# Mixing products of sixteen-head attentions: 32 streamed columns of values in place of 64

## The reference

```python
scores = jnp.einsum('bhqd,bhkd->bhqk', q, k) / np.sqrt(dk)
attn = jax.nn.softmax(scores, axis=-1)
o = jnp.einsum('bhqk,bhkd->bhqd', attn, v)
o = o.transpose(0, 2, 1, 3).reshape(B, S, D) @ Wo
```

## Time and profile before

| what | value |
|---|---|
| median of 3 runs | 5153.12 us (5146.67 to 5158.76) |
| span of the profiled execution | 5152.4 us |
| own time of the profiled execution | not listed apart; span and median differ by 0.7 us |
| PE busy, share of the span | 4143.7 us, 80% |
| DVE, POOL, ACT busy | 2973.1, 2418.9, 2100.3 us |
| mean granted TensorE clock | 0.892 of full speed |
| all mixing matmuls (L719) busy | 766.1 us |

### The profile page before, as it was taken

How to read it: one execution, slowest core, us unless ns; L and a number is a source line. 1 busy time by engine, 2 the same in 40 slices (tenths; PEclk the granted TensorE clock), 3 DMA queues, 4 the chain that set the end, 5 groups by cost and what they waited for, 6 DMA issues and landing times. The chain is left out here.

```text
span 5152.4 us, 287025 instructions
## 1 busy us (share of the span) xinstructions
PE 4143.7 (80%) x120907; PEld 3282.4 (64%) x120916; DVE 2973.1 (58%) x10848; ACT 2100.3 (41%) x5737; POOL 2418.9 (47%) x4370
## 2 busy tenths in 40 slices
PE   7998987255799987656898997749878998889988
PEld 6887764133576776523777885425547887778866
DVE  4555548532344478787554553863335657776656
ACT  3554445111343445365454555112224543345622
POOL 3443432177333477587333442028874446655510
PEclk9999998655899989856999998869998999999989
DMA  3000001333100022200000001114431000000000
GB/s 90 5 5 18 18 16 54 75 65 61 38 0 0 11 38 38 38 1 1 1 0 10 19 19 50 41 40 76 76 61 32 0 9 18 17 10 1 0 10 25
DMA packets 380523, 139.90 MB, mean 27 GB/s; under 512 B 216486, under 2 KB 373238, under 8 KB 380054
## 3 DMA queue, kind: packets, MB, share of 16 engines
q1 hardware_dynamic: 345430, 107.60, 8.8%
q0 software_dynamic: 34816, 28.34, 3.8%
HBM read 91.46 MB, written 43.85 MB: 26 GB/s over the span
## 5 line engine op out<-in xcount | busy, mean ns | idle before, releaser
L1049 DVE TENSOR_REDUCE rowmax<-ps 128x16 f32<-128x1024 f32 x512 | 626.9, 1224 | 732.3 <-PE ps L676 732.3
L695 PE MATMUL ps<-qT,kblock 32*64 32x64 f32 x36864 | 946.5, 229 | 45.1 <-issue 39.1
L695 PEld LDWEIGHTS ps<-qT,kblock 32*64 32x64 f32 x36864 | 779.9, 134 | 94.2 <-issue 44.0
L676 PE MATMUL ps<-kblock,qT 32*64 32x128 f32 x16384 | 790.6, 291 | 17.5 <-issue 17.2
L899 ACT ACTIVATE probT<-ps 128x1024 f32<-128x1024 f32 x512 | 523.3, 1022 | 675.4 <-PE ps L706 675.4
L719 PE MATMUL ps<-v,probT 64*64 64x64 f32 x36864 | 766.1, 228 | 3.0 <-ACT probT L899 1.6
L561 POOL TENSOR_TENSOR vareps<-moments,eps 128x1 f32<-128x1 f32 x521 | 100.9, 194 | 1411.1 <-DVE negmean L1023 1411.1
L719 PEld LDWEIGHTS ps<-v,probT 64*64 64x64 f32 x36864 | 684.4, 141 | 96.9 <-issue 88.0
L585 POOL TENSOR_TENSOR kblock<-kT,key_scale 128x512 f32<-128x512 f32 x576 | 600.2, 1042 | 39.2 <-ACT kT L877 26.1
L676 PEld LDWEIGHTS ps<-kblock,qT 32*64 32x64 f32 x16384 | 469.4, 135 | 153.4 <-issue 129.2
L886 ACT ACTIVATE xn<-x_res,nmr,rstd 128x128 f32 (+1 forms) x512 | 253.0, 494 | 419.6 <-POOL nmr L567 329.1
(11 more groups left out here) (379 smaller groups left out, 9404.8 us busy)
## 6 DMA issues: line engine op xcount, KB each, us to landing
ctxT<-in_ctxT SPq DMA_DIRECT2D x256, 64.0 KB, 1.8
held<-in_g_w SPq DMA_DIRECT2D x16, 836.0 KB
ctxT<-in_ctxT SPq DMA_DIRECT2D x256, 32.0 KB, 1.8
table<-prob SPq DMA_DIRECT2D x32, 256.0 KB, 2.4
x_dram<-x_res SPq DMA_DIRECT2D x32, 256.0 KB, 2.3
x_res<-x_dram SPq DMA_DIRECT2D x16, 512.0 KB, 7.2
x_res<-in_x SPq DMA_DIRECT2D x8, 512.0 KB, 7.9
x_res<-in_e_w SPq DMA_DIRECT2D x64, 64.0 KB
```

What stands on the lines that cost most here:

```text
L676: mm = nc.tensor.matmul(k.s1[S * b:S * b + S, g % 2, at:at + 2 * S].rearrange("p (h s) -> p h s", h=2), k.qT[rows, buf, S * b:S * b + S], ...
L695: mm = nc.tensor.matmul(out, k.kblock[rows, buf, h, S * b:S * b + S], k.qT[rows, buf, S * b:S * b + S], start=not part.softmax or (first a ...
L1049: nc.vector.tensor_reduce(spread, heads, AX.X, ALU.max).then_inc(soft.did["max_raw"], 1)
```

## The change

The moving operand and the output of each mixing product are cut to the first 32 columns. The stationary operand, the order, the number of products and all waits stay.

```diff
 NB = 3
+MOVED = 32
...
-                mm = nc.tensor.matmul(k.ps_o[S * b:S * b + S, u, S * hh:S * hh + S],
+                mm = nc.tensor.matmul(k.ps_o[S * b:S * b + S, u, S * hh:S * hh + MOVED],
                                       k.probT[rows, buf, at:at + S],
-                                      k.v9[rows, buf, (HD + 1) * h:(HD + 1) * h + S],
+                                      k.v9[rows, buf, (HD + 1) * h:(HD + 1) * h + MOVED],
                                       start=True, stop=True, tile_position=(S * r, S * b))
```

## The result

The changed kernel takes 5317.77 us (median of 4 runs, 5305.21 to 5324.43); the kernel before took 5149.9 us beside it (4 runs). The ratio is 1.0317, 95% interval 1.029 to 1.0344: 3.2% slower. The forecast was slower, at 6150 us, with 5380 us as its lower end. The direction and the cause (lost clock) held. The growth was 168 us and not 997: the step that the plain stages don't come back to the upper level failed.

The account below looks back on a forecast made before the run. The prediction took a PE-DVE-PE circle containing the mixing burst to set the step. Seven stages at the lower clock for their whole length added 997 us: 5152.4 + 997 + 0.7 = 6150 us, range 5380 to 6360.

Parts of the forecast that it names:

- the step that the plain stages don't come back to the upper level: Stages without added rows whose clock falls at their start would stay at 0.50, with 7.70 us steps.
- The burst's pace: In the mixing burst, weight loads set the pace, so the body keeps its length, 0.94 us; halved stream costed at nothing.
- the shorter drain: At the burst's end, the last product streams 0.027 us less, letting scores start sooner: 7 us over four stages.
- The third rival: In the mixing burst, streaming is the pace and the burst halves: 211 us less, 4940 us; chance 0.02.
- The clock: On PE, fewer streamed columns cost granted clock, though PE's busy share is unchanged; stages fall to 0.50: +997 us.
- The second rival: On PE, the clock doesn't notice because the engine is as busy as before: only 7 us saved, 5146 us; chance 0.07.
- The prices at the lower level: Steps at clock 0.50: plain 7.70 us, L1_xattn 7.22 less 0.05 us, L3_xattn 8.4 us.
- the terms +139, +179, +149, +147 and +143: In these five stages, us added if each runs its whole length at clock 0.50.
- L3_xattn's +172: L3_xattn at 0.50 throughout: 64 steps of 8.4 us, 538 us against 366.1.
- mean streaming of whole steps: Plain steps at 0.50 would stream 0.33 a us; steps from which the clock returned had 0.38, or 0.36 in L1_xattn.
- the returns held burst records: Before clock returns, the stretches looked at held part of a mixing burst or were full of the front; one held 44 records.
- Rival 1: Plain stages come back since the front is dense enough; only L1_xattn and L3_xattn stay down: 5386 us; chance 0.18.

Follow-up runs that it names:

- thin repeats: Changed kernel (32 columns) plus query projections repeated with 8 columns each, four in L1_xattn and two in the other stages: 6364.11 us, ratio 1.2343.
- 8-column repeats: Kernel before (64 columns) plus four repeats of the query projection in each L1_xattn step, each passing 8 columns: 5151.81 us, ratio 0.9998.
- the version with two wide stages: Changed kernel with 64 columns given back to L1_xattn and L3_xattn, 32 in the other seven attentions: 5197.23 us, ratio 1.008.
- the one with L0_attn kept wide: Changed kernel, 32 columns only in steady loops, 64 in L0_attn, L1_xattn, L3_xattn, and four query-projection repeats in L1_xattn: 5154.03 us, ratio 0.9998.

## Why the prediction was wrong in size, and what held

**The burst's pace: right.** The halved stream was costed at nothing, from the 8-column records of the earlier trace rows. Bursts of 1.16, 1.13 and 1.12 us show it. The small gain by the shorter drain was right too: plain steps went from 5.11 to 5.09 us. The third rival rests on what the Trainium skill says (TensorE: Matmul & The Clock Gate, in its section on what happens when a matmul is issued), that throughput is purely the number of columns streamed. The trace doesn't agree for this burst, where each product has a load of its own: half the columns took 1.13 us and not half of 1.16.

**The clock: right.** The loss is granted clock: it lies in the stages that lost clock; giving the wide product back to two stages gives their clock back; streaming for nothing in PE's pauses gives it back as well; being busy doesn't. The second rival read what the Trainium skill says of the gate (TensorE: Matmul & The Clock Gate, in its part on the HAM clock gate), that it is set by how busy the PE has recently been, as the busy share of the profile. The stage that was busy for 531.19 of 536.90 us at 0.50 refutes that reading.

**The prices at the lower level: right.** Plain step 7.70 forecast, 7.71 measured. L1_xattn +68 forecast, +63.8 measured. L3_xattn's step was put at 8.4 us; at 0.50 the changed kernel has 4578.00 - 4569.73 = 8.27:

```profile
4569.73 3.63 PE L720 MATMUL ps<-v,probT 64*64 64x32 f32 x64
4578.00 3.63 PE L720 MATMUL ps<-v,probT 64*64 64x32 f32 x64
```

**The step that failed: "a stage whose clock falls at its start doesn't come back".** It was named there as the weakest. With 32 columns the plain stages do come back, after stretches such as 47.7 us at the start of L0_attn (the windows of the changed kernel):

```profile
88.00:135.70 47.70, 47.32 (x1257) 44.34 (x1258) 18.23 (x65) 18.07 (x60) 14.76 (x32) 0.50 0.05 7
135.70:360.00 224.30, 207.71 (x9065) 186.47 (x9063) 129.50 (x440) 122.12 (x399) 102.83 (x221) 1.00 0.01 3
```

So the terms +139, +179, +149, +147 and +143 for L0_attn, L0_xattn, L2_xattn, L3_attn and L3_ffn, 757 us together, came out as +18.6, -2.4, +9.3, +0.5 and +4.8, 31 us. L3_xattn's +172 became +53: it isn't down throughout but goes down and up. By its mean clock it spends 54% of its time at 0.50 ((1 - 0.73) / 0.5). I had compared mean streaming of whole steps (0.33 against 0.36 and 0.38 a us) and read a limit into a gap that the trace didn't measure. The other argument, that the returns held burst records, doesn't hold either. The 3.4 us before one return in L3_xattn of the changed kernel held two mixing records (window of L720: length, PE, PEld, clock, DMA):

```profile
4409.20:4412.60 3.40, 0.05 (x2) 0.05 (x2) 0.50 0.00 0
```

Rival 1 said that the front, which isn't touched, is dense enough by itself. Returns at 32 columns fit that, but at 16 columns, and with steps lengthened by thin repeats, the front is there as well and the plain stages don't come back; so the failure was one of degree. Rival 1's sum wasn't right either: it kept L3_xattn down throughout (+172 for +53) and gave the plain stages no loss. That its 5386 us lies nearer is in part luck.

Two smaller slips. The row of L3_xattn in the earlier trace rows ends one burst early, so its term should have been 538 - 373.6 = +164. And the upper end of 6360 us doesn't follow from the bounds named with it: 6150 + 135 is 6285, 6150 + 179 is 6329. Nothing in the result hangs on either.

**Open.** What exactly the chip counts stays open. What brings a fall or a return wasn't measured; only that with 32 columns the returns come later, and with 16 in the plain stages not at all. Why the 8-column repeats did L1_xattn no harm is not settled. Why stages with added rows (L0_xattn, L1_attn, L2_attn) hardly suffer, even with 16 columns, was not tried apart; the added rows are the one group that the plain steps lack.

## What to carry to other kernels

Before cutting work that is hidden on TensorE, read the granted clock by stage: where it lies below 1.00 or PE has regular pauses, the columns that a wasteful matmul streams may be what holds the clock up, and cutting them can cost far more than it saves. Here matmuls with their own load of weights were hardly made faster by fewer moving columns: 64, 32 and 16 took 1.16, 1.13 and 1.12 us for 64 records. Where PE waits in each step anyway, a repeated product into the same place can be worth trying: four of them in L1_xattn gave 0.3%. Where the pause is short it costs time: two repeats made plain steps 0.1 us longer on average.

## What the runs showed of the hardware that was not expected

The loss is steep. When a plain stage fell to the lower level in its first 60 us, it was back within 17 us in every profile with 64 columns there, after up to 78.5 us with 32 (L3_ffn in the version with two wide stages, below), and with 16 L2_xattn and L3_ffn didn't come back in 480 us, though one group of matmuls alone had changed.

```profile
4644.10:4722.60 78.50, 78.14 (x2076) 73.38 (x2077) 39.53 (x169) 33.81 (x97) 27.93 (x65) 0.50 0.01 3
```

Versions with 32 columns in the loops vary more from run to run: the one with L0_attn kept wide ranged over 49 us in 12 runs (5131 to 5180), the kernel before over 32 us in 29 runs on the same chip. The version with repeats and 64 columns ranged over 20 us in 9.

The granted clock in a profile can be missing at its start, as in the changed kernel until 70.9 us. With 16 columns L0_attn is shown at 1.00, though its 64 steps took 502.7 us, 7.9 each, which is the pace of the lower level:

```profile
33.90:536.60 502.70, 494.88 (x13132) 466.14 (x13130) 188.80 (x642) 182.62 (x569) 152.13 (x319) 1.00 0.06 12
```
